# Plain attention of a vision tower: which queue issues the four transfers of the score maxima

## The reference

```python
q = jnp.einsum('bshd,hed->bshe', xh, Wq) + bq[None, None]
k = jnp.einsum('bshd,hed->bshe', xh, Wk) + bk[None, None]
v = jnp.einsum('bshd,hed->bshe', xh, Wv) + bv[None, None]
att = jax.nn.softmax(jnp.einsum('bshd,bthd->bhst', q, k) / jnp.sqrt(jnp.float32(D_HEAD)), axis=-1)
msa = jnp.einsum('bhst,bthd->bshd', att, v).reshape(n, SEQ, HIDDEN_D)
return tokens + msa
```

## Time and profile before

| | us |
|---|---|
| runs | 5170.82, 5178.77, 5185.15; median 5178.77 |
| the profiled execution, its own time | 5181.33 |
| its span, first to last instruction | 5179.6 |

### The profile page before, as it was taken

How to read it: one execution, slowest core, us unless ns; L and a number is a source line. 1 busy time by engine, 2 the same in 40 slices (tenths; PEclk the granted TensorE clock), 3 DMA queues, 4 the chain that set the end, 5 groups by cost and what they waited for, 6 DMA issues and landing times. The chain is left out here.

```text
span 5179.6 us, 168455 instructions
## 1 busy us (share of the span) xinstructions
PE 4742.6 (92%) x54416; PEld 3964.3 (77%) x54484; DVE 3282.0 (63%) x7845; ACT 2859.8 (55%) x7044; POOL 2024.9 (39%) x3205
## 2 busy tenths in 40 slices
PE   6999997888988889889869999999999899989988
PEld 6999997566766667667658888888888566669965
DVE  5777776566666666666646666666666588860057
ACT  4666664455555555555524555555555588864445
POOL 4666664244444443443422222222222355541145
PEclk9999998788898788887869999999999999999965
DMA  5777776455565555555546666666666222239977
GB/s 166 234 236 232 233 236 194 114 152 149 145 158 147 147 149 146 153 148 148 147 99 124 132 129 131 132 132 128 132 132 131 62 86 87 85 98 275 276 217 231
DMA packets 655747, 809.75 MB, mean 156 GB/s; under 512 B 223023, under 2 KB 514765, under 8 KB 655662
## 3 DMA queue, kind: packets, MB, share of 16 engines
q1 hardware_dynamic: 655662, 808.66, 61.0%
HBM read 518.94 MB, written 285.18 MB: 155 GB/s over the span
## 5 line engine op out<-in xcount | busy, mean ns | idle before, releaser
L703 DVE TENSOR_REDUCE a_mx<-a_sq 99x4 f32<-99x788 f32 x768 | 749.6, 976 | 538.9 <-PE a_sq L749 534.0
L644 ACT ACTIVATE a_ex<-a_sk 99x792 f32<-99x792 f32 (+1 forms) x768 | 637.7, 830 | 443.8 <-PE a_sk L766 434.7
L1118 DVE TENSOR_REDUCE c_mx<-c_sq 99x2 f32<-99x198 f32 (+1 forms) x1536 | 656.3, 462 | 267.3 <-PE c_sq L1172 253.2
L1070 ACT ACTIVATE c_ex<-c_sk 99x792 f32<-99x792 f32 (+1 forms) x768 | 511.0, 665 | 340.1 <-PE c_sk L1202 233.7
L400 PE MATMUL e_tokp<-e_wmap,e_pa 128*99 128x192 f32 x3072 | 453.8, 259 | 38.0 <-POOL e_pb L296 38.0
L766 PE MATMUL a_sk<-a_qs,a_ks 50*99 50x198 f32 (+1 forms) x3072 | 349.3, 309 | 139.0 <-DMA a_qs<-a_mxp 136.3
L1008 POOL CAST c_mxp<-c_mxr 12x198 bf16<-12x198 f32 x128 | 43.2, 338 | 1036.1 <-DVE c_mxr L1125 1036.1
L400 PEld LDWEIGHTS e_tokp<-e_wmap,e_pa 128*99 128x99 f32 x3072 | 396.9, 167 | 38.0 <-issue 38.0
L1169 PE MATMUL c_sq<-c_maskb,c_identb 99*99 99x198 bf16 x1536 | 383.2, 261 | 43.7 <-DVE c_bout L1108 30.2
L606 POOL CAST a_parts<-a_rest 96x396 bf16<-96x396 f32 x256 | 130.6, 510 | 737.8 <-DVE a_rest L726 737.8
L766 PEld LDWEIGHTS a_sk<-a_qs,a_ks 50*99 50x99 f32 (+1 forms) x3072 | 226.3, 185 | 250.7 <-issue 110.0
(11 more groups left out here) (198 smaller groups left out, 12430.4 us busy)
## 6 DMA issues: line engine op xcount, KB each, us to landing
scr_qk<-e_parts SPq DMA_DIRECT2D x128, 594.0 KB
e_patches<-in_x SPq DMA_DIRECT2D x128, 588.0 KB
x_w<-in_fc SPq DMA_DIRECT2D x128, 576.0 KB, 5.5
a_qs<-scr_qk SPq DMA_DIRECT2D x768, 74.2 KB
a_ks<-scr_qk SPq DMA_DIRECT2D x768, 74.2 KB
scr_qk<-a_parts SPq DMA_DIRECT2D x128, 445.5 KB
scr_tv<-e_tv SPq DMA_DIRECT2D x128, 297.0 KB
a_tv<-scr_tv SPq DMA_DIRECT2D x128, 297.0 KB
```

The costliest lines, as they stand in the source:

```text
L644: nc.scalar.activation(ex[0:rows, g, kt].rearrange("p (a s) -> p a s", a=2), sk[0:rows, :, 0:2 * SP], ACT.Exp).then_inc(exped.sem, 1)
L703: nc.vector.reduce_max(mx[:, b2.parity, qt].rearrange("p (r h) -> p r h", r=2)[:, :, 2 * g:2 * g + 2], sq[:, :, 0:2 * SP].rearrange("p r ( ...
L1070: nc.scalar.activation(to, of, ACT.Exp).then_inc(exped.sem, 1)
L1118: nc.vector.reduce_max(mx[:, b2.parity, qt, h:h + 2], sq[f % 2][:, :, 0:width], AX.X).then_inc(maxed.sem, 1)
```

## The change

The four transfers and the wait ahead of them move from SyncE's step to ScalarE's step, behind the fourth exponentials (number 3) and ahead of the copy to `hT`. The transfers themselves, their semaphore and the one that waits for it stay as they were. The initial count of `max_in_place` is given by ScalarE instead of SyncE.

```diff
         @block.sync
         def _(sp):
-            for e in (qk_in_place, tv_in_place, max_in_place, stored):
+            for e in (qk_in_place, tv_in_place, stored):
                 e.seed(sp)
...
-                b = c - 3
-                if b.inside(n):
-                    sp.wait_ge(max_low.sem, max_low.at(b))
-                    for a in range(2):
-                        for r in range(2):
-                            row = HALF * r + KQ + a
-                            sp.dma_start(qs[row:row + 1, b.place].bitcast(F32), mxp[r * HC:(r + 1) * HC, b.parity, a].bitcast(F32)).then_inc(max_in_place.of(b), 16)
...
         @block.scalar
         def _(act):
-            for e in (max_copied, exped, o_copied, h_high, high, v_copied):
+            for e in (max_copied, max_in_place, exped, o_copied, h_high, high, v_copied):
                 e.seed(act)
...
                 sums(b5, 2)
                 exponentials(2)
                 exponentials(3)
+                if b3.inside(n):
+                    act.wait_ge(max_low.sem, max_low.at(b3))
+                    for a in range(2):
+                        for r in range(2):
+                            row = HALF * r + KQ + a
+                            act.dma_start(qs[row:row + 1, b3.place].bitcast(F32), mxp[r * HC:(r + 1) * HC, b3.parity, a].bitcast(F32)).then_inc(max_in_place.of(b3), 16)
                 if b7.inside(n):
```

## The result

The median after the change is **5349.27 us** (5343.33 to 5361.95), against 5179.57 us before in the same job (5170.82 to 5185.15): a ratio of 1.0332, with a 95% interval of 1.0308 to 1.0357. The profiled execution took 5343.33 us, with a span of 5341.6, where that of before took 5181.33: +162.0 us. The forecast was 5395.

What follows compares the result with a forecast made beforehand. In the attention stage, SyncE's queue and PE close a ring of about 12 us, with slow clock as second cost. Work 10.7, stall 1.9 and clock 2.5 make 15.1 us per step, +215 us: 5395 us, range 5330 to 5540.

Steps and rivals of the forecast that it cites:

- Work of 10.7 us per step: Plain attention stage: work and small gaps take 10.7 us of each 13.37 us step, without maxima waits and slow clock.
- The wait for the maxima goes, 1.07 us: PE's wait before the key scores for the moved transfers, 1.07 us per step on average, disappears.
- Four issues on ScalarE cost 3.2 us: ScalarE's queue: issuing the four transfers takes 3.2 us, as on SyncE, ahead of the copy `a_hT`.
- The issues start at GpSimd's end: ScalarE's four issues start within 0.2 us of GpSimd finishing the maxima, the wait for `max_low` being nearly free.
- Stall of 1.9 us per step: PE idles before the value products because `a_hT` is late: 1.9 us per step, taken between 1.4 and 2.3.
- Clock: PE's clock falls after stalls in 0.7 of steps instead of 0.45, each costing 3.6 us: 2.5 us per step.
- The sum: Stage step of 10.7 + 1.9 + 2.5 = 15.1 us instead of 13.37: +215 us over 124 steps, 5395 us.
- cheap issues on ScalarE: Rival: four issues on ScalarE turn out short and SyncE is relieved, 4885 or 5085 us; chance 0.12.
- A stall with the clock up: Rival: PE stalls before the value products as computed, clock stays up; step 13.0 us, 5133 us; chance 0.03.
- a fall after every stall: Rival: slow clock follows each PE stall; step 16.2 us, 5530 us; no separate chance, part of the forecast's range.
- Slow clock no more often than before: Rival: PE stalls 2.1 us, slow clock still costs 1.6 us; step 14.4 us, 5307 us; chance 0.17.
- The rule for balancing issues: Skill's rule that spreading DMAs over issuing engines may help where one is solid with them; it spoke against the forecast.

Runs made afterwards that it cites:

- e2: Changed kernel without the four maxima transfers and their waits, their rows in `qs` zeroed once: 4871.93 us, ratio 0.9385 to the kernel before.
- e3: Kernel before, SyncE keeping its four transfers, plus four like them issued by ScalarE at the change's place into an unread buffer: 5375.69 us, ratio 1.0354.
- e6: Kernel before with the three stores of an image issued by ScalarE behind the second exponential, maxima transfers still on SyncE: 4900.54 us, ratio 0.9467.
- e1: Kernel before with two of the four transfers issued by ScalarE at the change's place, two left on SyncE: 5170.19 us, ratio 0.9952.
- e4: Changed kernel with the four issues one instruction later, behind ScalarE's copy for `a_hT`: 5135.96 us, ratio 0.9899 to the kernel before.
- e5: Kernel before, all issues on SyncE, reordered: four maxima transfers first, then tv load, stores a step later, q and k loads last: 5147.01 us, ratio 0.993.
- e9: Kernel before with the three stores on ScalarE as in e6, but at the change's place, behind the fourth exponential: 5210.5 us, ratio 1.0053.
- e8: e6 plus two of the four transfers (low parts) on ScalarE behind the copy to hT: 4899.51 us, ratio 0.9461 to the kernel before.

## Why the prediction was right, step by step

- **Work of 10.7 us per step**: right, 10.87 measured in e2.
- **The wait for the maxima goes, 1.07 us**: right; 0.8 us is left in the whole stage.
- **Four issues on ScalarE cost 3.2 us**: right. 677 ns each at the median, 675 on SyncE; the groups of four run from 2.80 to 3.9 us, with a mean of 3.14. This term carried the forecast. It was chosen between 0 and 1.7 us each without any row of ScalarE, on the ground that the same transfer should cost the same: a good guess, not a reading. e3 shows that it alone makes the loss.
- **The issues start at GpSimd's end**: the step that was off. They start 0.01 us after the fourth exponential does, in 127 of the 128 groups, and that is 0.18 to 1.22 us after GpSimd's end (median 0.26), not within 0.2. So in this step at half clock of after, beside the earlier trace rows:

```profile
1500.28 0.60 POOL L592 TENSOR_TENSOR a_mxp<-a_mxr,a_mxp 12x198 fp32r<-12x198 f32 x1
...
1502.02 0.83 ACT L637 ACTIVATE a_ex<-a_sk 98x792 f32<-98x792 f32 x1 [1.26 <-PE a_sk L765]
...
1502.02 2.80 ACTq L664 DMA_DIRECT2D a_qs<-a_mxp  x4
...
1504.92 0.66 ACT L668 CAST a_hT<-a_wb 128x594 fp32r<-128x594 f32 x1 [2.07 <-PE a_wa L839]
...
1506.49 0.88 PE L776 MATMUL a_wb<-a_ex,a_vx 99*32 99x198 f32 x16 [1.25 <-issue]
```

  GpSimd was done at 1500.88, the issues begin at 1502.02, 1.14 us later: they stand behind the exponential, and that waits for PE's key scores. I had let a step at half clock hide them but for 0.3 us; in fact it stalls PE 1.25. The copy L668 starts 0.10 us after the last issue. That its row names PE's L839 misleads: the copy waits for those products of an earlier image only, and before the change it started at 1540.48 in the midst of them (they ran from 1539.84 to 1542.78).
- **Stall of 1.9 us per step**: 279.3/127 = 2.2. Of the 118 steps of the stage but for five at either end, 100 had the issues at full clock and stalled PE 2.0 to 3.1 us, 2.44 in the mean, where I had 2.3 and let the slow stretch of the step before take part of it off; 18 had them at half clock and stalled it 1.2 to 1.4 us instead of 0.3.
- **Clock**: the number of falls was right, their length too large. Between 1000 us and the end of the stage, the granted clock was low in 58 stretches of 8.7 us on average before (0.48 per step) and in 84 of 7.2 us after (0.70 per step, as forecast). I had priced each at 10.3 us, from one 12 us window. The mean clock is 0.82, not 0.77: (1 - 0.82) x 2 x 14.77 = 5.3 us of a step at the lower level, x 0.35 = 1.9 us instead of 2.5. The price of 0.35 is from one step; by difference from e2 it is 14.77 - 10.87 - 2.2 = 1.7 us, so 0.32. That it is waits that bring the clock down rests on the kernels side by side: no fall in e2, one in e6 with waits of 0.45 us per step and 1.4 at most, 0.33 to 0.70 falls per step in before, after, e1 and e4, whose waits go up to 1.9 or 3.1 us. Two windows of after, the one up to the stall of 3.11 us and the one behind it:

```profile
1506.00:1519.00 13.00, 10.52 (x164) 7.96 (x164) 7.77 (x10) 6.71 (x13) 5.54 (x10) 1.00 0.52 134
1520.00:1532.00 12.00, 11.68 (x112) 8.36 (x112) 6.74 (x9) 5.75 (x11) 5.63 (x10) 0.55 0.55 136
```

- **The sum**: with the measured terms 10.9 + 2.2 + 1.9 = 15.0 us per step, 14.77 measured, 15.1 forecast. The mechanism held; that the number came within 1% is in part luck, as the stall was put 0.3 us too low and the clock 0.6 too high. Against the forecast's +1.73 x 124 = +215 us stand +1.40 x 127 = +177 in the stage; the +162 of the profiled executions is that less the 15 us outside it, which lie within what executions of one kernel differ by.
- **The rivals**: cheap issues on ScalarE are excluded by the 677 ns. A stall with the clock up (5133) and a fall after every stall (5530) are excluded by 0.70 falls per step. "Slow clock no more often than before" (5307) is as near to the 5349 measured as the forecast's 5395: it had less clock (1.6 us, measured 1.7 to 1.9) for the wrong reason, as falls came more often and were shorter.
- **The rule for balancing issues**, the first rival: the Trainium skill ("Perfetto Trace Analysis", DMA Optimizations) says that balancing them may help where an issuing engine is solid with them; it holds here only with the right transfers at the right place. SyncE's queue was the limit, as e6 shows by 5.3%. Moving the maxima to the change's place lost 3.3%.

Why groups of the same four transfers take 2.8 us at one time and 3.9 at another follows the 445.5 KB store of `scr_qk`, which SyncE issues. In after, with the ends of the stage left out, the 34 groups begun 0.1 to 0.4 us ahead of its issue took 3.4 to 3.9 us (the first step above: 1514.81 and 1514.96), the 43 begun 0.7 to 1.7 us after it 2.8 to 3.6, and the 35 begun 1.8 us or more after it 2.80 to 2.82. By single issues: those on ScalarE begun 1 to 2 us after the store's took 1.05 us in the mean, those begun 3 us or more after it 0.68. It is not a matter of one queue: there the store is SyncE's and the long issues ScalarE's, in e6 the other way round (loads on SyncE 1.28 us instead of 0.34), in e5 both are SyncE's (1.33 instead of 0.34). No run takes the store away, and two smaller stores always go just ahead of it, so this is an order in time and not a shown cause. In e3 two groups side by side took 3.48 and 2.91 us.

Left open: what in the large store does this, and the third way to issue the four, from GpSimd's queue, which was not tried.

## What to carry to other kernels

Moving a transfer's issue to another engine moves its full issue time, here 0.68 us each, in front of whatever stands next in that engine's order; look at that instruction and who waits for it, not at the engine's idle share. Take off a full queue what nobody waits for soon, here three large stores rather than four small urgent transfers, and put it ahead of an instruction that waits anyway: the same three issues gave 4900 or 5210 us by their place. Waits of PE can cost twice, once as themselves and once as the clock behind them, so reckon a removed wait at more than its length: e6 took 0.62 us of waiting out of a step (1.07 to 0.45), and the step became 2.15 us shorter.

## What the runs showed of the hardware

- An issue costs ScalarE what it costs SyncE (677 and 675 ns for the same transfer), and its length does not follow the bytes: the store of 445.5 KB took 0.34 us to issue, each of the four transfers of 4.6 KB 0.68.
- An issue on ScalarE does not wait for the arithmetic ahead of it to end (1514.81 with the exponential of 1514.80), nor even for it to start (e4: 1520.91 with the copy of 1521.55 ahead of it). But it does not pass an exponential that still waits for its input: 1502.02, with its own input ready at 1500.88.
- Issues begun 1 to 2 us after that of the 445.5 KB store took 1.05 to 1.33 us in the mean instead of 0.34 or 0.68, whether store and issue were on one queue (e5) or on two (after, e6).
- With the stores issued beside them, the small transfers reached PE 4.31 us after the last issue at the median instead of 1.59 (e9 against e6). That the stores are the reason is not shown: with the four spread over both queues it was 3.40 us in e1 and 3.15 in e8.
